# Whole-weight operations of the opening attention: in halves, behind each step's own work, and one of them on GpSimd

## What is computed

```python
x = x + xattn0(layernorm(x), ctx)   # 16 heads of 64; Wq, Wk, Wv: 256x1024, Wo: 1024x256
x = x + ffn0(layernorm(x))          # ternary weights, int8 rows, depthwise conv, silu
x = x + xattn1(layernorm(x), ctx)   # 16 heads of 16, rms norm and rotary on q and k
x = x + ffn1(layernorm(x))          # int8 weights, uint8 activations, one scale over all rows
```

## Time and profile before

| | |
|---|---|
| median of 3 runs | 2360.57 us (2360.05 to 2366.0) |
| the profiled execution | 2361.02 us, its span 2359.2 us |
| mean granted TensorE clock | 0.995 |
| busy share of PE, DVE, ACT, POOL | 97%, 74%, 67%, 72% |

### The profile page before, as it was taken

The page is one execution under the profiler, slowest core; times in us unless marked ns, Lnnn a source line. Parts: engine busy times, 40 slices in busy tenths (PEclk is TensorE's granted clock), DMA queues, the critical chain, the costliest instruction groups (busy, mean ns, idle before and its releaser), DMA issues.

```text
span 2359.2 us, 62966 instructions
## 1 busy us (share of the span) xinstructions
PE 2286.8 (97%) x20874; PEld 1830.5 (78%) x20874; DVE 1743.7 (74%) x4342; ACT 1587.5 (67%) x4467; POOL 1691.7 (72%) x1863
## 2 busy tenths in 40 slices
PE   7999999999999999999999999999999999999788
PEld 6778877778788777778877778787777878877546
DVE  5777777787777777777777777777778777778785
ACT  6666666776667677666766766666677666667356
POOL 2777777777777777777787777777777777877607
PEclk9999999999999999999999999999999999999899
DMA  4000000000000000000000000000000000001202
GB/s 147 10 11 10 10 8 10 2 10 10 10 10 9 10 2 10 10 10 10 10 8 9 4 10 10 10 10 8 10 2 10 10 10 10 8 4 36 57 11 63
DMA packets 31472, 37.06 MB, mean 16 GB/s; under 512 B 3301, under 2 KB 29653, under 8 KB 31445
## 3 DMA queue, kind: packets, MB, share of 16 engines
q1 hardware_dynamic: 31444, 36.71, 5.3%
HBM read 29.36 MB, written 7.34 MB: 16 GB/s over the span
## 4 chain that ended last, share of the span: by engine, by line
PE 88%; DVE 4%; ACT 4%; issue 3%; POOL 2%; DMA 0%; POOLq 0%; ACTq 0%; SPq 0%; DVEq 0%
PE ps L367 25%; PE pt L471 11%; PE ps L447 10%; PE pa L483 7%; PE pt L461 5%; PE ps L411 5%; PE pa L523 4%; PE pa L498 4%; ACT probT L828 3%; PE ps L435 2%; PE pa L367 2%; PE pt L367 2%; PE pa L633 1%; PE ps L426 1%; DVE th L1547 1%
## 5 line engine op out<-in xcount | busy, mean ns | idle before, releaser
L1145 DVE TENSOR_REDUCE nmx<-ps 112x2 f32<-112x750 f32 x512 | 478.2, 934 | 142.2 <-PE ps L447 91.4
L1643 POOL TENSOR_TENSOR prob<-prob,rinv 112x375 f32<-112x375 f32 x512 | 404.2, 810 | 130.3 <-DVE rinv L1153 130.2
L1643 POOL TENSOR_TENSOR prob_last<-prob_last,rinv 112x375 f32<-112x375 f32 x512 | 411.9, 830 | 59.1 <-DVE rinv L1153 59.0
L828 ACT ACTIVATE room<-ps 128x376 f32<-128x376 f32 (+2 forms) x480 | 227.5, 487 | 265.9 <-PE ps L367 265.9
L828 ACT ACTIVATE probT<-pt 125x336 f32<-125x336 f32 (+1 forms) x512 | 242.6, 474 | 167.8 <-PE pt L461 112.5
L868 ACT ACTIVATE prob<-ps,nmx 112x375 f32<-112x375 f32 x512 | 289.9, 581 | 65.0 <-DVE nmx L1145 65.0
L868 ACT ACTIVATE prob_last<-ps,nmx 112x375 f32<-112x375 f32 x512 | 290.7, 584 | 8.2 <-DVE nmx L1145 8.2
L1670 POOL TENSOR_TENSOR krs<-krs,nhalf 125x48 f32<-125x48 f32 x32 | 257.0, 8030 | 0.0
L1136 DVE COPY probT<-pt 125x336 f32<-125x336 f32 x322 | 161.9, 503 | 97.4 <-PE pt L471 97.3
L483 PE MATMUL pa<-probT,room 125*64 125x112 f32 x3072 | 183.0, 265 | 0.0
L471 PEld LDWEIGHTS pt<-ident,prob 112*125 112x125 f32 x966 | 118.5, 189 | 72.7 <-issue 64.2
(11 more groups left out here) (294 smaller groups left out, 5981.0 us busy)
## 6 DMA issues: line engine op xcount, KB each, us to landing
craw<-in_ctx SPq DMA_DIRECT2D x32, 375.0 KB, 3.1
xin<-in_x SPq DMA_DIRECT2D x32, 112.0 KB, 2.0
x_rows<-x SPq DMA_DIRECT2D x32, 112.0 KB, 1.9
out<-probT SPq DMA_DIRECT2D x16, 224.0 KB, 2.3
room<-x_rows SPq DMA_DIRECT2D x1, 2576.0 KB, 13.7
w<-in_f1w SPq DMA_DIRECT2D x2, 1024.0 KB, 6.6
stage<-in_wk SPq DMA_DIRECT2D x2, 512.0 KB, 4.7
stage<-in_wv SPq DMA_DIRECT2D x1, 1024.0 KB, 7.5
```

The costliest lines, as they stand in the source:

```text
L828: return act.activation(dst, src, ACT.Copy)
L1145: top = dve.tensor_reduce(nmx[:, g:g + 2], ps[0:T, 2 * (i % 2):2 * (i % 2) + 2, 0:S], AX_X, ALU.max, negate=True)
L1643: pool.tensor_tensor(prob(i, n), prob(i, n), rinv[:, g:g + 1].to_broadcast([T, S]), ALU.mult).then_inc(s["normed"], 1)
```

## The change

The operations on the second weight, and some on the first, are cut in two instructions over halves of the columns, and they stand at other places of the streams. PE's weight sum adds the two halves' sums in two products. The subtraction for `wo0_lo` is whole, and POOL does it, behind the last pair of the opening and ahead of `rest`.

| operation | before | after |
|---|---|---|
| first weight: shift (ACT) | step 1 | half ahead of exponentials 0, half behind exponentials 1 |
| second weight: sum (DVE) | step 1 | halves in steps 1 and 2 |
| weight sum (PE) | step 2, behind turning | step 3, behind turning |
| scale (DVE) | step 2 | step 3 |
| round (ACT) | step 3, at its start | halves at the ends of steps 3 and 4 |
| clip (DVE) | step 4 | step 5 |
| shift (ACT) | step 5, at its start | halves at the ends of steps 5 and 6 |
| `wo0_hi` (ACT) | step 6, at its start | halves at the ends of steps 6 and 7 |
| `wo0_lo` | DVE, step 7 | POOL, behind its pair 7 |

```diff
+        halves = [slice(n * DC * F // 2, (n + 1) * DC * F // 2) for n in range(2)]
 # PE
-                    if part == OPENING and i == 2:
+                    if part == OPENING and i == 3:
                         weight_sum(1)
-                pe.matmul(pa[:, 1, n:n + 1], ones[:], wmean[:, n:n + 1], start=True, stop=True)\
-                    .then_inc(s["wsum_done"], 1)
+                cols = ((0,), (1, 4))[n]
+                for c in cols:
+                    last = pe.matmul(pa[:, 1, n:n + 1], ones[:], wmean[:, c:c + 1], start=(c == cols[0]),
+                                     stop=(c == cols[-1]))
+                last.then_inc(s["wsum_done"], 1)
 # ACT
-                    if part == OPENING and i in (1, 5):
-                        weight_shift(i // 5)
-                    if part == OPENING and i == 3:
-                        weight_round(1)
-                    if part == OPENING and i == 6:
-                        act.wait_ge(s["wo0_in"], 16)
-                        copy(wo0_hi[:], stage[1].rearrange("p (c n) -> p c n", c=IC)).then_inc(s["wo0_hi"], 1)
...
                     elif part != CLOSING:
                         kv1_copy(k, i - (count - 2))
+                    if part == OPENING and i in (3, 4):
+                        weight_round(1, i - 3)
+                    if part == OPENING and i in (5, 6):
+                        weight_shift(1, i - 5)
+                    if part == OPENING and i in (6, 7):
+                        output_upper(i - 6)
...
+            def output_upper(half):
+
+                act.wait_ge(s["wo0_in"], 16)
+                ins = copy(flat(wo0_hi, F32R)[:, halves[half]], stage[1][:, halves[half]])
+                if half == 1:
+                    ins.then_inc(s["wo0_hi"], 1)
...
-            weight_round(0)
+            for half in range(2):
+                weight_round(0, half)
             v0_copy(0, [4, 5])
+            weight_shift(0, 0)
             for i in range(AHEAD):
                 exps(i, OPENING, 0)
+            weight_shift(0, 1)
             attention(OPENING, 0)
 # DVE
+            def weight_half(half):
+
+                dve.wait_ge(s["f0w2_in"], 16)
+                ins = dve.tensor_reduce(wmean[:, (1, 4)[half]:(1, 4)[half] + 1], stage[0][:, halves[half]], AX_X, ALU.add,
+                                        apply_absolute_value=True)
+                if half == 1:
+                    ins.then_inc(s["wsum_ready"], 1)
...
-                    if part == OPENING and i == count - 1:
-                        dve.wait_ge(s["wo0_hi"], 1)
-                        dve.tensor_tensor(wo0_lo[:], stage[1].rearrange("p (c n) -> p c n", c=IC), wo0_hi[:].bitcast(F32),
-                                              ALU.subtract).then_inc(s["wo0_lo"], 1)
-                    if part == OPENING and i in (1, 2, 4):
-                        ternary(1, (1, 2, 4).index(i))
+                    if part == OPENING and i in (1, 2):
+                        weight_half(i - 1)
+                    if part == OPENING and i in (3, 5):
+                        ternary(1, (i - 1) // 2)
 # POOL
             attention(OPENING, 0, 0, PAIRS)
+            pool.wait_ge(s["wo0_hi"], 1)
+            pool.tensor_tensor(wo0_lo[:], stage[1].rearrange("p (c n) -> p c n", c=IC), wo0_hi[:].bitcast(F32),
+                               ALU.subtract).then_inc(s["wo0_lo"], 1)
             with pool.Fori(0, B - 1) as b:
                 rest(b, False)
```

More of the change, by code:

```diff
@@ L870, in exps, with weight_shift @@
                 ins.then_inc(s["exped"], 1)
-            def weight_shift(n):
+            def weight_shift(n, half):
                 act.wait_ge(s["w_clip"], n + 1)
-                act.activation(flat((f0w1, f0w2)[n], BF16), stage[1 - n], ACT.Identity, bias=whole[:, 1:2])\
-                    .then_inc(s["w_quant"], 1)
+                ins = act.activation(flat((f0w1, f0w2)[n], BF16)[:, halves[half]], stage[1 - n][:, halves[half]],
+                                     ACT.Identity, bias=whole[:, 1:2])
+                if half == 1:
+                    ins.then_inc(s["w_quant"], 1)
             def kv1_copy(b, t):
@@ L1003, in rest, with weight_round @@
                         exps(i, CLOSING, b)
-            def weight_round(n):
+            def weight_round(n, half):
                 act.wait_ge(s["w_scale"], n + 1)
-                act.activation(stage[1 - n], stage[1 - n], ACT.Identity, bias=whole[:, 0:1],
-                               scale=wmean[:, (3, 6)[n]:(3, 6)[n] + 1]).then_inc(s["w_round"], 1)
+                w = stage[1 - n][:, halves[half]]
+                ins = act.activation(w, w, ACT.Identity, bias=whole[:, 0:1], scale=wmean[:, (3, 6)[n]:(3, 6)[n] + 1])
+                if half == 1:
+                    ins.then_inc(s["w_round"], 1)
+            def output_upper(half):
+                act.wait_ge(s["wo0_in"], 16)
+                ins = copy(flat(wo0_hi, F32R)[:, halves[half]], stage[1][:, halves[half]])
+                if half == 1:
+                    ins.then_inc(s["wo0_hi"], 1)
             act.wait_ge(s["wk0_in"], 16)
```

## The result

The changed kernel takes 2367.4 us (median of 20 runs, 2366.33 to 2370.09) against 2361.03 for the kernel before (20 runs, 2360.03 to 2368.59). The ratio of the two is 1.0022, with a 95% interval of [1.0015, 1.0029]. It is formed over all the runs, and so is not the quotient of the two medians (1.0027); either way the change loses, by 0.2 to 0.3%. The profiled execution's span is 2364.8 us against 2359.2.

A forecast was written before the change was run, and what follows sets the result against it. PE bounds the kernel (busy 97%), except in the opening, where whole-weight operations on DVE and ACT do. Profiled 2361.02 + 5.4 (5.3 POOL queue, 0.1 rounding) + 1.5 clock = 2367.9; median 0.45 lower, 2367.5; range 2363.3 to 2370.5, own range 2365.3 to 2369.

The forecast's parts named there:

- POOL's subtraction: Output weight's rest, on POOL in the opening: 4.5 us from about 59.6; PE idle some 3.6 us for it.
- the low half: Context's low half on POOL, behind subtraction and two key tiles: ready 70.45, PE waits 3.5 us before the third key term.
- the upper part: Output weight's upper part on ACT, in halves: second half ends at 59.55, against 54.93 before.
- the walk: Row-by-row times through the opening from row maximum 2: second key/value product done at 57.6 instead of 59.5, 1.9 us gained.
- the rounding in two halves: First weight's rounding on ACT in two instructions, ahead of the value copies: costs about 0.1 us.
- The clock behind the third term: PE at 1.2 GHz for some 3 us after 70.5, behind its waits: about +1.5 us, bounds 0 and 3.5.
- rival 1: Further low clock stretch between 42 and 56 delays the second key/value product by 1.2 to 2.5: 2369.5 us, chance 0.20.
- Rival 2: Shorter POOL chain: POOL takes 4.2 or ACT is free a microsecond sooner; +2 to +3.5, no clock loss: 2363.5, chance 0.13.
- Rival 3: Second key/value product alone decides, 1.9 us sooner; upper part ready by 54.2 or POOL operation free: 2358.7, chance 0.05.

The follow-up runs named there:

- experiment 2: Kernel before, with only the subtraction for the output weight's rest moved from DVE to POOL, all whole-weight operations whole and at old places: 2360.84 us, ratio 0.9988.
- experiment 5: Changed kernel plus useless products on PE, 18 before the wait for the output weight's rest, 12 behind the output product's first half: 2369.04 us, ratio 1.0023.
- experiment 3: Changed kernel with the output weight's upper part whole again at the start of ACT's step 6, subtraction still on POOL: 2361.57 us, ratio 1.0002.
- experiment 1: Changed kernel with the output weight's subtraction back on DVE, behind its squares of key tile 1; halves and places stay: 2361.06 us, ratio 0.9986.
- experiment 6: Changed kernel with first weight rounded whole, subtraction on DVE between key tiles' squares, weight sum, clip and second upper half moved: 2359.89 us, ratio 0.9983.

## Why the prediction was right, and where it was lucky

**The mechanism held at each link.** POOL's subtraction took 4.51 (forecast 4.5). PE waited for it 3.78 (3.6), and then for the low half. From the upper part to the third term the forecast had 70.5 - 59.55 = 10.95, and the changed kernel's two traces and experiments 2 and 5 have 10.9 to 11.0. DVE stood 2.72 ahead of the clip (2.5). PE's work between the two waits did run at 1.2 GHz and took 4.5 us instead of 2.9, and the second wait did cover it: it shrank from the forecast's 3.5 to 1.79.

**The upper part was 1.9 us later than forecast** (61.45 against 59.55), and with it went the 1.9 us that the walk had gained up to the second key/value product: that product ended at 59.4 and not at 57.6, against 59.5 before. So in this pair of traces the halves gained next to nothing. The 1.9 has three parts.

- 0.46 was there at the first scores. Of it 0.28 is the rounding in two halves, 2.38 against 2.10 whole, and not 0.1 (ACT's timeline before, below); it stands at 28.8 us, outside the 36 to 66 that the prediction called the only stretch with changed code. The rest is no more than executions differ by: the three of the kernel before have their first scores at 31.53, 32.05 and 32.74.
- 0.70 is the clock, which fell at 52.7 us, behind PE's wait for DVE's late copy. A key/value product took 2.7 instead of 1.5. But little more than half of that went on to the upper part. In experiment 5's trace, where the clock happened to stay full here (its filling comes later), PE is done sooner and then waits 0.62 for ACT, and the upper part comes 28.76 us behind the first scores instead of 29.46.
- The other 0.74 is the walk itself. Halves of the rounding took 1.13 to the next start, not 1.0 (those of the shift 1.04, those of the upper part 0.95). The second half of the rounding ended at 49.75 and not at 48.8, and so about 0.5 of the 0.74 was there by then.

```profile
28.81 2.10 ACT L1008 ACTIVATE stage<-stage,whole,wmean 128x2048 f32<-128x2048 f32 x1 [2.10 <-DVE wmean L1231]
```
```profile
55.94 0.88 PE L473 MATMUL pt<-ident,prob_last 112*125 112x112 f32 x6 [0.62 <-ACT probT L841]
```

The walk did not have PE's wait of 0.64 at 47.66 either. The profile puts it down to POOL, but PE wants POOL's pair 4 there, which was done at 46.49; what ended just ahead of it is ACT's copy of pair 3 (47.03 + 0.48 = 47.51), which stood behind the first half of the rounding. The path to the upper part does not go through this wait: ACT and DVE are at the rounding and the clip meanwhile.

**The clock behind the third term** cost 1.31 (forecast 1.5); in experiment 5, with the waits filled, it is gone (72.45).

**The number was right partly by chance.** By the first traces the changed kernel is 8.5 us late at power 2, nearer to rival 1's figure (8.9) than to the forecast's 6.9. The closing gave 3.0 back in this pair. What the forecast did not allow for is that the trace before was one draw: a quick opening (33.63 where two others took 34.7 and 35.6) and a slow closing. Against the mean of the three openings, 34.7, the change costs 5.7 there and 1.3 behind it, 7.0 in all; the medians say 6.4 and 6.0 in the two sets. A walk that came out 1.4 too short behind the first scores and a baseline that was quick by 1.0 nearly cancel. The forecast's own range, 2365.3 to 2369, holds the 2367.4.

**Rivals.** Rival 1 is there in its mechanism, a low stretch between 42 and 56, but not in its size: it passed 0.70 on to the upper part, not 1.2 to 2.5. Rival 2 is out: POOL's operation had its proportional length, and ACT was later than forecast, not sooner. Rival 3 asked for the upper part at 54.2, or for a POOL operation that costs nothing, and promised 1.9 us of gain. Its direction was right: with the upper part at 56.8 and 56.2 (experiments 2 and 3) or with the subtraction off POOL (1) the loss is gone. Its gain is in none of the three, and its number was not reached by any.

## What to carry to other kernels

Before an operation goes to an idle engine, look at when its input is ready and not at how much idle time the engine has: here POOL had 6.4 us, all of it ahead of the input. Then read what stands behind it in that queue, to the next thing that the bound engine waits for, since a small operation deep in the queue (a 1.64 us subtraction, a 0.55 us inverse root) sets the price. And before an operation is cut in halves, look at who waits for the second half, and at what is queued behind that wait: here DVE stood 2.72 us for it with row maximum 7 behind.

## What the runs showed of the hardware

- *POOL and DVE can shut each other out.* While POOL's 4.51 us subtraction ran, DVE's operation on 48 columns took 2.98 us; in experiment 6, clear of POOL's longer operations, the same one took 0.23. Not every operation of DVE is shut out: during the same subtraction a copy out of PSUM took 0.51 and a sum over 256 columns 0.42, as elsewhere. The other way round, DVE's subtraction in experiment 1 stretched two products on POOL from 0.87 to 2.92. POOL's timeline of experiment 1, and then DVE's:

```profile
65.23 2.92 POOL L1690 TENSOR_TENSOR room<-room,ropk 125x128 f32<-125x128 f32 x2
```
```profile
64.99 2.43 DVE L1331 TENSOR_TENSOR wo_lo<-stage,wo_hi 128x2048 fp32r<-128x2048 f32 x1 [0.53 <-ACT wo_hi L833]
```

  The Trainium skill (SBUF — State Buffer, Who interferes with whom) describes an exclusive lock on a port pair, held for a whole instruction, for DVE operations with two SBUF inputs or in a two-port mode. The rows agree: the operation that came second waited for the first one's end (63.10 + 2.98 = 66.08 against 61.53 + 4.51 = 66.04). No row shows in which mode the 48-column operation ran, which has one input. The profile counts such a wait as busy time. In the changed kernel it was off the path; in experiment 6 it made all of PE's 1.58 us wait for the low half, and in experiment 1 the 0.24.
- *Executions of one kernel differ by where the low clock falls.* The same kernel took 33.6 to 35.6 us in the opening and 167.3 or 170.2 in the closing, and the 30 rounds between were 2051.4 to 2051.5 in all three. In the closing the low clock was as long in both cases, 13.7 us; it cost 3 us more where PE had no waits to hide it. So the opening read from one trace of this kernel is known to about 2 us.
